# New orders of the steps on every engine of a four-layer kernel

## What is computed

```python
# layer 0: low-rank conditional matrix; gated 8-expert attention; gated 8-expert MoE
x = x + L0_ffn(L0_cond(x, cond_8))
# layer 1: one expert of 8 per batch (argmax); MoE over 16 experts, each expert takes
# its 128 best tokens of every batch (top_k over the 256 tokens); layer norm
expert = jnp.argmax(opcode_onehot, axis=-1)
hidden = jax.nn.silu(up) * gate
_, seq_ids = jax.lax.top_k(route_e, max_len)
out = jnp.einsum('eblf,efd->ebld', jax.nn.gelu(h, approximate=False), w2) + b2
x = x + L1_ffn(L1_cond(x, cond_8))
# layer 2: two skills of 8 per batch and a shared one; soft MoE with 64 x 32 slots
logits = (jnp.einsum('tzd,ed->tze', x, phi_w) + phi_b).reshape(t, z, n, p)
D = jax.nn.softmax(logits, axis=3)
C = jax.nn.softmax(logits, axis=2)
X_tilde = jnp.einsum('tznp,tzd->npd', D, x)      # then norm, tanh, 64 experts: Y_tilde
Y = jnp.einsum('tznp,npH->tzH', C, Y_tilde)
x = x + L2_ffn(L2_cond(x, cond_8))
# layer 3: conditional matrix; 16-head attention with rope; shared and routed SwiGLU
w_bot = jnp.einsum('bg,got->bot', y, masked_w)
x = x + L3_ffn(L3_cond(x, cond_8))
```

## Time and profile before

| | us |
|---|---|
| median of 3 runs | 1142.11 (1142.01 to 1143.24) |
| span of the profiled execution | 1140.3 |
| PE busy | 1020.7 |
| DVE busy | 760.8 |
| ACT busy | 499.1 |
| POOL busy | 154.3 |

### The profile page before, as it was taken

The page is one execution under the profiler, slowest core; times in us unless marked ns, Lnnn a source line. Parts: engine busy times, 40 slices in busy tenths (PEclk is TensorE's granted clock), DMA queues, the critical chain, the costliest instruction groups (busy, mean ns, idle before and its releaser), DMA issues.

```text
span 1140.3 us, 18292 instructions
## 1 busy us (share of the span) xinstructions
PE 1020.7 (90%) x6790; PEld 763.6 (67%) x6790; DVE 760.8 (67%) x1828; ACT 499.1 (44%) x823; POOL 154.3 (14%) x164
## 2 busy tenths in 40 slices
...
GB/s 333 2 29 15 15 16 15 7 9 15 1 130 1 56 129 1 57 56 26 31 129 2 1 1 1 113 1 1 1 1 6 1 6 6 1 6 1 6 6 9
DMA packets 11800, 35.39 MB, mean 31 GB/s; under 512 B 2570, under 2 KB 5818, under 8 KB 10944
## 3 DMA queue, kind: packets, MB, share of 16 engines
...
q0 software_dynamic: 96, 0.04, 0.0%
...
## 4 chain that ended last, share of the span: by engine, by line
issue 42%; PE 41%; DVE 7%; POOLq 3%; ACT 3%; POOL 2%; DVEq 1%; ACTq 0%
PE ps L847 5%; PE ps L1147 5%; PE ps L1122 3%; PE ps L1298 3%; PE ps L1189 2%; PE ps L881 2%; PE ps L1209 2%; PE ps L857 2%; PE ps L1229 2%; PE ps L893 2%; PE ps L904 2%; POOLq L2153 1%; POOLq L2158 1%; PE ps L836 1%; DVE arena L1956 1%
## 5 line engine op out<-in xcount | busy, mean ns | idle before, releaser
L1975 DVE TENSOR_REDUCE arena<-ps 128x8 f32<-128x2048 f32 x32 | 73.2, 2288 | 27.1 <-PE ps L1189 27.0
L1506 ACT ACTIVATE arena<-ps 128x2048 f32<-128x2048 f32 x32 | 60.1, 1877 | 50.1 <-PE ps L1213 50.0
L1033 PE MATMUL ps<-arena,uR 128*128 128x512 f32 x128 | 68.8, 620 | 8.2 <-ACT arena L1451 7.9
L1122 PE MATMUL ps<-uR,arena 128*128 128x256 f32 x256 | 73.9, 385 | 0.0
L1058 PEld LDWEIGHTS ps<-arena 128*128 128x128 f32 x512 | 61.1, 191 | 6.6 <-issue 3.0
L1058 PE MATMUL ps<-arena 128*128 128x128 f32 x512 | 63.0, 276 | 2.0 <-DVE xacc L1898 1.2
L1298 PE MATMUL ps<-arena 128*128 128x512 f32 x128 | 61.7, 606 | 2.8 <-DVE xacc L2051 1.2
L1147 PE MATMUL ps<-arena 128*128 128x256 f32 x256 | 60.6, 384 | 3.2 <-DVE arena L1929 2.6
L1479 ACT ACTIVATE arena<-ps 128x512 f32<-128x512 f32 x64 | 37.8, 597 | 51.9 <-PE ps L1123 51.7
L847 PE MATMUL ps<-arena 128*128 128x256 f32 x256 | 58.3, 386 | 0.0
L1873 DVE TENSOR_REDUCE arena<-ps 128x16 f32<-128x512 f32 x64 | 44.3, 692 | 20.2 <-PE ps L1034 15.6
...
## 6 DMA issues: line engine op xcount, KB each, us to landing
...
```

The source lines that it names most:

```text
L1033: mm(high[:, c, :], uR[:, b, k * P:(k + 1) * P], phiC[:, col:col + 512], start=True, stop=False)
L1122: mm(o, phiC[:, st_ * P:(st_ + 1) * P], uR[:, b, :], start=True, stop=False)
L1506: av(pexp[:, t, gp].rearrange("p c h t -> p (c h t)"), scores[:, :, :].rearrange("p c t -> p (c t)"), ACT.Exp, scale=SCALE3).then_inc(s.sc ...
L1975: V.tensor_reduce(nm[:, k, :, 2 * gp:2 * gp + 2], scores[:, :, :].rearrange("p c (h t) -> p c h t", h=2), X, ALU.max, negate=True).then_in ...
```

## The change

Only ORDER_A and ORDER_BD change, on all five engines. Every list has the same words as before, in another sequence; steps, buffers, semaphores and waits are the same. (The table grows by a line, so lines behind it have a number that is one higher.) SP issued the two halves of layer 2's expert weights (EWA, EWB) behind the third and the seventh load of skills; now they and EBD stand behind all eight. The core of the difference, with the places that are spoken of below:

```diff
--- before.py
+++ after.py
...
-    LG3.0 MT2.0 BC1.3 SG3.1 SU3.1 SH2.0 SG4.1 Z.3 SG5.1 LG4.0 MT3.0 SU4.1 SH3.0 LG5.0 SU5.1 MT4.0 SH4.0 XT0.0 UC.1
-    MT5.0 LG6.0 UT.1 SH5.0 SG0.2 XT1.0 MT6.0 ZT.3 SG1.2 LG7.0 SU0.2 SH6.0 MT7.0 SG2.2 LG0.1 SU1.2 SH7.0 MC.0 BC0.4
...
+    SG2.1 LG2.0 SU2.1 LG3.0 SG3.1 MT2.0 SU3.1 SG4.1 SH2.0 Z.3 LG4.0 MT3.0 SU4.1 SH3.0 MT4.0 SG5.1 SH4.0 LG5.0 SU5.1
+    LG6.0 UC.1 MT5.0 XT0.0 MT6.0 UT.1 SH5.0 SG0.2 XT1.0 SG1.2 LG7.0 SG2.2 SH6.0 ZT.3 MT7.0 SU0.2 SH7.0 LG0.1 MC.0
...
-    SH2.0 SG4.1 SG5.1 MT3.0 SH3.0 MT4.0 SH4.0 MT5.0 UC.1 SH5.0 SG0.2 MT6.0 UT.1 SG1.2 SH6.0 ZT.3 MT7.0 SG2.2 SH7.0
...
+    MT2.0 SG4.1 SH2.0 MT3.0 MT4.0 SH3.0 SH4.0 SG5.1 UC.1 MT5.0 SH5.0 SG0.2 UT.1 SG1.2 MT6.0 SH6.0 MT7.0 ZT.3 SH7.0
...
-    X5T.0 NM.1 FF0.0 TS0.1 FF1.0 TS1.1 FF2.0 TS2.1 G3.0 FF3.0 V.2 TS3.1 CL0.3 AV0.1 AV1.1 CL1.3 CL2.3 CL3.3 CL4.3
...
+    SQ1.0 X5T.0 FF0.0 NM.1 TS0.1 FF1.0 S.2 TS1.1 FF2.0 FF3.0 V.2 TS2.1 TS3.1 G3.0 CL0.3 CL1.3 AV0.1 AV1.1 CL2.3
...
-    NM.0 X3.1 RQ.1 RK.1 CSUM.2 REC.2 MX0.1 SA0.0 CN0.2 CN1.2 MX1.1 SA1.0 CN2.2 MX2.1 CN3.2 MX3.1 NM.1 X5.0 X3.2 FH0.0
...
+    NM.0 X3.1 CSUM.2 RQ.1 RK.1 REC.2 CN0.2 MX0.1 SA0.0 CN1.2 SA1.0 MX1.1 CN2.2 MX2.1 X5.0 MX3.1 NM.1 FH0.0 CN3.2
...
-    RSZ.0 RSZ.1 RSZ.2 RSZ.3 W.0 W.1 WA.1 W.2 WA.2 W.3 RSZ.4 WA.3 RSZ.5 W.4 RSZ.6 RSZ.7 WA.4 W.5 WA.5 W.6 WA.6 W.7
...
+    W.0 W.1 WA.1 RSZ.0 RSZ.1 W.2 WA.2 W.3 WA.3 W.4 RSZ.2 WA.4 W.5 RSZ.3 WA.5 W.6 WA.6 RSZ.4 RSZ.5 RSZ.6 W.7 RSZ.7
...
```

More of the change, by code:

```diff
@@ L121 @@
[L121 to L125, removed]
@@ L143 @@
[L143 to L147 removed]
+    QK.1 NT0.2 VT.1 NT1.0 SC.1 LOG1.0 MH0.0 LOG0.2 PT.1 AT.1 MH1.0 GTR1.0 SPR1.0 O1.1 GTR0.2 MOE.0 NT1.1 COND.3
@@ L184 @@
-    SO.1 CL5.4 WO.2 MX3.3 CL6.4 RT0.1 CL7.4 NM.3 RT1.1 TS0.3 X5T.2 CSUM.4 RT2.1 TS1.3 G3.2 Y0.4 Y1.4 TS2.3 RT3.1 AV0.3
-    TS3.3 Y2.4 Y3.4 OUT.1 AV1.3 S.4 FF0.2 V.4 Q.4 FF1.2 AVT0.3 K.4 CL0.5 FF2.2 MX0.4 CL1.5 AVT1.3 CL2.5 MX1.4 FF3.2
-    SAT.3 CL3.5 CL4.5 MX2.4 WO.3 SO.2 CL5.5 MX3.4 RT0.2 CL6.5 CL7.5 NM.4 RT1.2 TS0.4 CSUM.5 X5T.3 RT2.2 G3.3 TS1.4
-    Y0.5 Y1.5 RT3.2 Y2.5 TS2.4 AV0.4 Y3.5 TS3.4 OUT.2 S.5 FF0.3 AV1.4 Q.5 V.5 FF1.3 K.5 CL0.6 AVT0.4 FF2.3 MX0.5
-    AVT1.4 CL1.6 CL2.6 MX1.5 SAT.4 FF3.3 CL3.6 CL4.6 MX2.5 WO.4 SO.3 CL5.6 MX3.5 RT0.3 CL6.6 CL7.6 X5T.4 NM.5 RT1.3
```

222 lines of the change are left out of this document (116 added, 106 removed).

## The result

The changed kernel takes 1102.86 us (median of four runs, 1102.56 to 1104.44) against 1142.67 for the kernel before in the same comparison: a ratio of 0.9655 [0.9637, 0.9674]. The profiled execution has a span of 1101.0 us, 39.3 less than before.

What follows compares the result with a forecast made beforehand. PE, busy 1020.7 of 1140.3 us, was taken as the bound, gains coming from its idle time and slow clock. Terms +1.2, 0, -5.5, -0.3, -12.8, +1.8 and +1.0 for new waits gave -14.6: 1127.5 us, range 1117 to 1138.

Steps and rivals of the forecast that it cites:

- Stage B: From 385 us to the join: MT7.0's wait and slow clock go, DVE takes part back; -5.5 us, bounds -2 and -9.
- the walk: Whole kernel: new order stepped through with step durations from the trace of before; source of all the sums.
- Start of D: 735 to 830 us: most of PE's 16.7 idle us and 1.7 of slow clock go; -12.8 us, the largest term.
- Three moves work together: Start of stage D: V.2 earlier on ACT, ACT steps paired for two fewer table loads, DVE's CSUM.2 earlier; together -12.8 us.
- D's interior and tail: Stage D after its start: DVE's G3 and GE steps between reductions lose some gain; +1.8 us, bounds 0 and +5.
- Stage A: First stage: small gains outweighed by new short waits; +1.2 us, within +-2.
- Route section: About 327 to 336 us: four POOL operations beside DVE's top-k rounds cost nothing; 0 us, other end +9.4.
- rival (2): Route section: port lock makes POOL block DVE's top-k loop by 9.4 us; 1137 us, chance 0.09.
- The join: 690 to 735 us: CN.0 still runs beside POOL's CSA and CSB; -0.3 us, bounds 0 and -2.
- Rival (1): Stages B and D: gains given back to DVE's load and PE's; 8 us gained, 1134 us, chance 0.18.
- Rival (3): Stages A, B, D: clock falls behind new short pauses, 1.7 us each; 1148 us with twelve, chance 0.08.
- Rival (4): Whole kernel: other steps replace the removed waits one for one, within 0.2%; 1142 us, chance 0.05.

Runs made afterwards that it cites:

- e2: Kernel before with every engine's new list for stage B up to the join, stages A and D old: 1123.41 us, 0.9837.
- e13: Kernel before with new PE, ACT and DVE lists from UC.2 to the join, plus POOL's new stage B list: 1131.0 us, 0.9899.
- e12: Kernel before with new PE, ACT and DVE lists from UC.2 to the join only, POOL's list old: 1137.66 us, 0.9957.
- e14: Kernel before with DVE's 32 multiplies for SH shortened to a sixteenth each, that computation missing, no list changed: 1135.51 us, 0.9939.
- e8: Kernel before with nine small swaps in PE's stage B list, most putting another step between SH and LG: 1147.16 us, 1.0053.
- e4: Kernel before with only POOL's stage B list in its new order: 1135.46 us, 0.995.
- e11: Kernel before with one DVE step moved, CSUM.2 ahead of RQ.1 and RK.1: 1142.19 us, 1.0005.
- e16: Kernel before with only the three moves named for the start of D (V.2 on ACT; CSUM.2 and SA1.0 on DVE): 1141.1 us, 0.9995.
- e17: Kernel before with new PE and ACT lists behind the join, DVE's and POOL's old: 1177.37 us, 1.0311.

## Why the prediction was wrong in size

**Stage B, −5.5 against −20.8: the step that failed.** Up to UC.2 the walk was right about the lists that it walked. Counted from ZT.0, UC.2 is 9.5 us earlier in e2 and 2.6 in e13, which differ by the new lists ahead of that place (and SP's); that makes 6.9, where the walk had 5.9. The step that failed is the next one, "what PE gains early, DVE's own work takes back in part". The walk had 4.4 to 4.75 us left at 481 to 511 and, with 1 us for the casts, 5.5 at B's end; the trace goes on from −11.4 at UC.2 to −22.7. Three things in it were wrong.

First, the taking back was argued from DVE's 84%. e12 has the new lists of PE, ACT and DVE behind UC.2 alone, and they gain 4.4 us there; e14 takes 32 us of work away from DVE, and 6.6 come back, so a busy share of 84% left room. Second, the prediction priced MT7.0's long wait and left the first row of B's wait list, 7.9 us in ten waits for ACT, out of the sum; with it, and the 3.3 us of SU, the short waits of B come to 18.7 us (7.9 + 7.5 + 3.3). That B's time fell by about as much is an observation; e8 shows that waits of this kind are not separate items to be struck off one by one. Third, POOL's moves were priced at about 1 us through two casts, although, from which the prediction itself had worked out 5.7 + 2.4 us of stretching, was at hand; alone they brought 6.6; by e4's trace 2.5 us are gained around MT7.0, whose wait the prediction had given to the order of PE and DVE while naming the POOL operation beside it, and 2.4 at the casts at 572 to 587 us. A walk with durations as they were cannot see that a stretched operation gets shorter.

MT7.0 starts at 415.41, without a wait, where the walk had 419.8 (1.9 us of the difference were there before B began):

```profile
415.41 0.23 PE L1042 MATMUL ps<-identb,arena 128*128 128x128 bf16 x1
```

What is shown: POOL's list brings 6.6 us alone and 11.2 in the company of the other lists; the other lists together bring the rest; the table loads and the cover on PE alone bring nothing, and of work taken off DVE a fifth comes back. Which property of the joint lists makes it work behind UC.2 stays open.

**Start of D, −12.8 against −14.4: right in size, the reason only in part.** PE's idle time there falls to 5.4 us, as worked out (16.7 less 11.7), and K.2 runs at 783.17 without a wait and at full clock:

```profile
783.17 1.13 PE L1175 MATMUL ps<-sqC,arena 128*128 128x256 f32 x4
```

V.2 on ACT is worth 3.2 us alone (0.1 to 3.9), of the 4.6 given to K.2. CSUM.2's move takes away SAT.0's wait and CSUM.2's own, 2.2 us, but not AVT1.0's 3.2, which was to shrink with them; all three moves together bring nothing that can be measured, partly because of the lower clock behind AVT1.0 in e11 and e16. The number was right because the walk had all the lists in it. The reason given for it, "Three moves work together", left out the rest of them, PE's own among them, without which AVT1.0's wait stays (3.1 in e11, 4.3 in e16; at most 0.7 in the kernel after). How much of the rest each list holds stays open.

**D's interior and tail, +1.8 against −2.5.** The walk found GE.2 in a hole that is too short; the trace has PE busy 97.83 of 98 us there. The sentence "The steady state of D can give nothing" was nearly true (1.5 idle us in 100 became 0.2); over the rounds from TS0.2 to TS0.5 it comes to 2.0 us. e17 shows how much the other sign could have been.

**Stage A, +1.2 against −1.8:** alone it measures 0, within the bounds of ±2; the −1.8 stands in e2 as well, with the old lists, so neither sign is shown. **Route section, 0 against −0.1:** right. POOL's four operations run beside DVE's rounds (POOL in order of time, the first and the last):

```profile
325.56 2.36 POOL L2153 TENSOR_TENSOR w3raw<-w3raw,mask 128x1024 f32<-128x1024 f32 x1
...
332.37 2.35 POOL L2160 TENSOR_TENSOR wb<-wb,arena 128x1024 f32<-128x1024 f32 x1
```

and MAX8 and MATCH_REPLACE keep the 0.43 and 0.41 us that they had before (DVE by line, as above):

```profile
L1816 DVE MAX8 arena<-arena 128x8 f32<-128x256 f32 x16 | 6.9, 429 | 1.6 <-issue 0.4
...
L1818 DVE MATCH_REPLACE8 arena<-arena 128x256 f32<-128x256 f32 x16 | 6.6, 409 | 0.0
```

So the row of the memset was the right one to take, and rival (2) fell. The Trainium skill (SBUF — State Buffer, section "SBUF: two separate sides") has the lock against GpSimd only for DVE operations in a 2-port mode or with two SBUF inputs. MAX8 has one input, and the trace agrees with the rule, provided that MAX8 is in no 2-port mode, which no row shows. **The join, −0.3 against +0.3:** right; CN.0 kept its company. **Rival (1),** that gains are given back, fell with the result. **Rival (3),** the clock, shows in the kernel after in the join (0.92 over 22 us, 1.8 us) and in none of the stretches of the earlier trace rows more than before, but it ate part of what e2, e11, e13 and e16 had won. **Rival (4)** fell with the result, though e8 shows that it can happen when one list is changed alone.
